# Cosine and sine products of one token tile, made in one interleaved run of matmuls instead of one after the other

## The reference

```python
def _rfs(xw, ab, AB, gs):
    dot_products = einsum('...d,rd->...r', xw, ab[:, None] * gs)
    correction = (0.5 * sum(xw * xw, axis=-1))[..., None] * (ab * ab)
    return 1.0 / sqrt(NUM_RFS) * AB * exp(dot_products - correction)
# layer 1
weights = _rfs(input_weights, ab, AB, proj_matrix)
feats = _rfs(x, ab, AB, proj_matrix)
x = layernorm(x + einsum('bsr,or->bso', feats, weights))
# layer 2
real = einsum('bti,io->bto', x, cos(theta + theta_noise))
imag = einsum('bti,io->bto', x, sin(phi + phi_noise))
x = layernorm(x + sqrt(real * real + imag * imag))
```

## Time and profile before

| | |
|---|---|
| median of 3 runs | 796.34 us (795.47 to 796.83) |
| span of the profiled execution, first to last instruction | 795.6 us |
| PE busy | 752.5 us (95% of the span), 3376 matmuls |
| DVE, ACT, POOL busy | 494.5, 366.4, 168.4 us |
| mean granted TensorE clock | 0.980 of full speed |

### The profile page before, as it was taken

One profiled execution on the slowest core, in us unless ns is written; L12 is line 12 of the kernel. 1 busy time (PEld: TensorE's weight loads), 2 busy tenths in 40 slices (PEclk: granted clock), 3 DMA queues, 4 the chain that ended last, 5 costly groups with the idle time before them and its releaser, 6 DMA issues.

```text
span 795.6 us, 10365 instructions
## 1 busy us (share of the span) xinstructions
PE 752.5 (95%) x3376; PEld 616.7 (78%) x3376; DVE 494.5 (62%) x874; ACT 366.4 (46%) x649; POOL 168.4 (21%) x300
## 2 busy tenths in 40 slices
PE   6567898999999999999999999999999999999995
PEld 5455687888888887888888887887888888888884
DVE  4288785574657557475756747574664747576464
ACT  6353644636263553526255452626445362634322
POOL 0386230120303012120301212030211203021122
PEclk9879999999999999999999999999999999999998
DMA  8663004040230403021030403104040301301001
GB/s 278 89 242 119 1 28 146 21 143 9 70 102 26 145 26 145 13 87 71 26 145 26 145 13 118 40 27 145 26 145 13 147 12 38 134 26 40 27 28 53
DMA packets 42062, 62.33 MB, mean 78 GB/s; under 512 B 11712, under 2 KB 11712, under 8 KB 42048
## 3 DMA queue, kind: packets, MB, share of 16 engines
q1 hardware_dynamic: 42048, 62.17, 24.2%
HBM read 45.35 MB, written 16.81 MB: 78 GB/s over the span
## 4 chain that ended last, share of the span: by engine, by line
PE 64%; DMA 21%; DVE 7%; ACT 4%; issue 2%; SPq 1%; POOL 0%; DVEq 0%; POOLq 0%; ACTq 0%
PE token_ps L470 14%; PE token_ps L468 14%; PE token_ps L469 14%; DMA token_norms<-norm_col 14%; DMA norm_bc<-token_norms 6%; PE project_ps L455 5%; PE project_ps L456 4%; PE project_ps L457 4%; PE token_ps L494 3%; PE token_ps L492 3%; PE token_ps L493 3%; PE turn_ps L500 2%; DVE expo L567 1%; DMA x_tok<-in_w 1%; ACT unused L316 1%
## 5 line engine op out<-in xcount | busy, mean ns | idle before, releaser
L280 POOL TENSOR_TENSOR var_eps<-mv,eps 128x1 f32<-128x1 f32 x128 | 39.7, 310 | 577.0 <-DVE mv L650 576.8
L388 ACT ACTIVATE late<-token_ps 128x512 f32<-128x512 f32 x128 | 76.1, 596 | 133.2 <-PE token_ps L470 132.8
L492 PE MATMUL token_ps<-W_hi,F_hi 128*128 128x512 f32 x256 | 100.7, 393 | 15.8 <-DVE F_lo L562 15.8
L382 ACT ACTIVATE zT_hi<-turn_ps 128x512 fp32r<-128x512 f32 x64 | 37.3, 585 | 166.6 <-PE turn_ps L500 166.6
L455 PE MATMUL project_ps<-xT_hi,gs_hi 128*128 128x512 f32 x248 | 102.7, 414 | 5.9 <-DVE expo L567 5.4
L468 PE MATMUL token_ps<-cos_hi,zT_hi 128*128 128x512 f32 x256 | 102.3, 400 | 3.1 <-DVE cos_lo L562 3.1
L470 PE MATMUL token_ps<-cos_hi,zT_lo 128*128 128x512 f32 x256 | 100.7, 393 | 0.0
L494 PE MATMUL token_ps<-W_hi,F_lo 128*128 128x512 f32 x256 | 100.4, 392 | 0.0
L493 PE MATMUL token_ps<-W_lo,F_hi 128*128 128x512 f32 x256 | 100.4, 392 | 0.0
L469 PE MATMUL token_ps<-cos_lo,zT_hi 128*128 128x512 f32 x256 | 100.3, 392 | 0.0
L468 PE MATMUL token_ps<-sin_hi,zT_hi 128*128 128x512 f32 x256 | 99.8, 390 | 0.0
(11 more groups left out here) (88 smaller groups left out, 1273.8 us busy)
## 6 DMA issues: line engine op xcount, KB each, us to landing
xT_raw<-in_xT SPq DMA_DIRECT2D x16, 1024.0 KB, 7.8
x_tok<-in_x SPq DMA_DIRECT2D x16, 1024.0 KB, 9.6
out_tokens<-o_tile SPq DMA_DIRECT2D x64, 256.0 KB, 2.9
norm_bc<-token_norms SPq DMA_DIRECT2D x17, 256.0 KB, 5.1
trig<-in_gsT SPq DMA_DIRECT2D x4, 256.0 KB, 4.7
z<-in_wT SPq DMA_DIRECT2D x4, 256.0 KB, 4.9
x_tok<-in_w SPq DMA_DIRECT2D x1, 1024.0 KB, 7.7
trig<-in_theta_noise SPq DMA_DIRECT2D x4, 256.0 KB, 6.5
```

The source lines that it names most:

```text
L388: nc.scalar.activation((re2, im2)[part][:, j % 2, :], token_ps[(2 * j + part) % 4][:, :], ACT.Square).then_inc(square_done, 1)
L492: nc.tensor.matmul(o, F_hi[:, c, cols], W_hi[:, c, :], start=(c == 0), stop=False)
```

## The change

In the steps 1 to 14 (the loop `pe.Fori(1, NB - 1)`) the eight phase products are issued as four pairs. `phase_pair(j)` goes over the chunks c once and issues for each the cosine and sine matmuls that have the same chunk of the turned tile as the stationary operand: four with `zT_hi`, two with `zT_lo`. Two PSUM banks are open at once. The semaphore `phase_done` is still raised twice a tile, by the last two matmuls. The pair waits once for what its two banks need. Step 0 and the last step keep the order of before; no other engine's code is changed.

```diff
+                def phase_pair(j):
+                    k = 2 * j % 4
+                    re_ps, im_ps = token_ps[k][:, :], token_ps[k + 1][:, :]
+                    pe.wait_ge(zT_made, C * b + j + 1 + TURN_CREDIT)
+                    if j < 2:
+                        pe.wait_ge(y_made, C * b + 2 * j + 2)
+                    else:
+                        pe.wait_ge(square_done, 2 * C * b + SQUARE_CREDIT + 2 * j - 2)
+                    for c in range(C):
+                        s, stop = slice(c * P, (c + 1) * P), c == C - 1
+                        nc.tensor.matmul(re_ps, zT_hi[:, j, s], cos_hi[:, c, :], start=(c == 0), stop=False)
+                        nc.tensor.matmul(re_ps, zT_hi[:, j, s], cos_lo[:, c, :], start=False, stop=False)
+                        nc.tensor.matmul(im_ps, zT_hi[:, j, s], sin_hi[:, c, :], start=(c == 0), stop=False)
+                        nc.tensor.matmul(im_ps, zT_hi[:, j, s], sin_lo[:, c, :], start=False, stop=False)
+                        last_re = nc.tensor.matmul(re_ps, zT_lo[:, j, s], cos_hi[:, c, :], start=False, stop=stop)
+                        last_im = nc.tensor.matmul(im_ps, zT_lo[:, j, s], sin_hi[:, c, :], start=False, stop=stop)
+                    last_re.then_inc(phase_done, 1)
+                    last_im.then_inc(phase_done, 1)
...
-                    for j, part in PHASE_ORDER_FIRST if first else PHASE_ORDER:
-                        phase(j, part)
+                    if first:
+                        for j, part in PHASE_ORDER_FIRST:
+                            phase(j, part)
+                    else:
+                        for j in range(C):
+                            phase_pair(j)
```

## The result

The changed kernel takes 812.63 us (median of 4 runs, 812.33 to 815.48) against 795.90 us for the kernel before in the same comparison (4 runs): a ratio of 1.0226, 95% interval 1.0200 to 1.0251 (an estimate from all the runs; the two medians alone give 1.0210). It is slower, by 16.7 us. Its profiled execution took 812.33 us and has a span of 810.5 us, 14.9 us more than the 795.6 of before. A run over 1.5% slower than the fastest of its kernel is left out everywhere; there was one, of 837.41 us, in the changed kernel's repeat further down.

The account below looks back on a forecast made before the run. The norms' trip through DRAM was taken to bind each step; 13 x 1.2 = 15.6 us plus 1.1 us for the last step gave a span of 812.3, plus 0.7 a forecast of 813.0 us, range 807 to 820.

Parts of the forecast that it names:

- The bound: Once a step PE waits for DVE's exponent behind the norms' trip, about 0.45 us; anything added to the trip lengthens the step.
- the norms' trip: Token norms stored to DRAM and broadcast back for DVE's exponent before project(2): store 9.93 us, load 3.36 us.
- The matmuls at 0: On PE, the new operand order and alternating banks cost 0; matmuls stay 0.227 us apart, 96 a step.
- The signal: Tile 3's cosine is ready only one matmul before sine, making output tile 1 and the norms' store 1.23 us later.
- PE's wait: PE's stand for the exponent each step, put at about 0.45 + 1.2 = 1.65 us.
- One side remark: DVE, later by the same 1.23 us, would take that delay out of its idle 2.66 us before the exponent.
- The sum: 13 trips at 1.2 us plus 1.1 us in the last step: 16.7 us on a span of 795.6, giving 812.3.
- 13 x 1.2 = 15.6: Trips behind the paired phase parts of steps 1 to 13, each lengthened by 1.2 us: 15.6 us.
- The last step: No norms there, but DVE's statistics, z and the first turn come later: +1.1 us.
- Rival 1, the clock: PE's longer stall lowers the granted clock, 1.46 us each time: 832 us in all 13 steps; chance 0.08.
- Rival 2: The norms' trip is not the last wait or shortens by as much: 796 to 800 us; no change, chance 0.05.
- Rival 3: More PE matmuls in a row with one stationary tile run faster, 786 us at 20 ns each; chance 0.04 for faster.

Follow-up runs that it names:

- the changed kernel's repeat: The changed kernel measured once more, unchanged, on the chip of a later batch: 825.12 us, ratio 1.0237 to the kernel before.
- taking the wait away: The kernel before, products apart, with DVE making output tile 1 earlier, ahead of the residual of tile 2: 793.83 us, ratio 0.9823.
- with the pairs: The changed kernel with output tile 1 made early on DVE and ACT's root moved behind the next tile's copy and sum: 794.47 us, ratio 0.9864.
- tile 3 taken back: The changed kernel with tile 3 alone back to cosine and then sine, tiles 0 to 2 still pairs: 807.97 us, ratio 0.9999.
- the cosine ahead by three: The changed kernel with each pair's last chunk issuing three cosine, then three sine matmuls: 820.64 us, ratio 1.0153 to the kernel before.
- norms first, apart: The kernel before with the token norms' store issued ahead of output tile 1's store on SP: 824.98 us, ratio 1.0216.
- norms first, pairs: The changed kernel with the token norms' store issued ahead of output tile 1's store on SP: 841.3 us, ratio 1.0403 to the kernel before.
- one signal in tile 3: The kernel before, matmuls in old order, tile 3 alone signalling cosine and sine together with its last sine matmul: 830.31 us, ratio 1.0327.
- one signal: The kernel before, matmuls in old order, every tile of steps 1 to 14 signalling both products with its last sine matmul: 833.59 us, ratio 1.0309.

## Why the prediction was right

It named 813.0 us, and 812.63 was measured. By its steps:

- **The bound.** That the norms' trip binds in each step held in both directions: 1.23 us more of it gave about 1.1 us a step, and taking the wait away gave a step of 45.45 us where it was 45.95 (12 steps from the mix at 155.07 to that at 706.49 us).
- **The matmuls at 0.** The distance is 0.227 us in the pairs, and the step without waits takes 45.45 us with the products apart and 45.45 to 45.61 with the pairs. The rule of the Trainium skill that I weighed ("TensorE: Matmul & The Clock Gate", on one weight load for many matmuls) has nothing to work on here: the profile has as many weight loads after as before, 3376.
- **The signal.** Output tile 1 was rebuilt at 3.35 us after the mix's first matmul (250.41 - 247.06), and stands at 3.35. The store of the norms came 1.23 us later, as rebuilt. The late signal alone, in tile 3 alone, reproduces the loss; tile 3 taken back removes it. PE's wait was put at 1.65 us a step, some 22 us in all, and is 20.1 us for the weight loads, 1.55 a step. One side remark was wrong: DVE did not take its delay out of its idle time ahead of the exponent, which is 2.75 us (2.66 before), because the landing it waits for moved as far.
- **The sum.** 13 x 1.2 = 15.6 was one term; the profile gives 14.1 us of idle time. The term is 1.1 us a step, not 1.2: between store and exponent the 13 trips took 13.33 us on average instead of 13.47 (from the start of the store to the start of the exponent, each of the 13). Why they were shorter stays open. The last step was put at +1.1 and is 1.54 - 0.41 = 1.13. Together 15.2, with the 0.2 given back at the start about the 14.9 of the spans. So the forecast span of 812.3 us was 1.8 too long. The time was reached from it by adding 0.7, the distance of the earlier median from one span, while the profiled execution's own time is 1.8 above its own span (812.33 and 810.5). The two errors partly cancel, so that the forecast missed by only 0.4 us is in part luck; by the spans the change cost 14.9 us, a tenth less than the 16.7 forecast.
- **Rival 1, the clock.** It did not happen in the steps 2 to 14 on the first chip, where the wait was 1.6 us at the longest, but the mechanism is real: in the kernels whose longest matmul wait was 2.2 us or more it struck in some steps, mostly at about the price given (1.46 us). A chance of 0.08 was fair for the first chip and perhaps low for that of the repeat, where the changed kernel waits up to 2.3 us and the clock fell in one step of the 13.
- **Rival 2** had hardly any ground: the trip was last in all 13 steps, and shortened by 0.14 us, not by 1.2. **Rival 3**, a gain from the shared stationary tile: none.

## What to carry to other kernels

When two products are interleaved so that they end together, the first one's result comes late by nearly the whole of the second, even if PE's own time is unchanged; ask what was done under the second one's matmuls. An engine that is 95% busy may still be held in each round by a trip of small transfers through DRAM; it shows in the chain that ended last and in a row of waits whose count is the number of rounds. And before a DMA is moved ahead of another, look up which buffer the second one frees, and when.

## What the hardware showed that I had not expected

- A 256 KB store issued 0.86 us behind the 2 KB store of the norms on the same queue was released 11 us after its issue, where the run's median is 2.9. The 2 KB store itself takes 8.0 to 11.6 us from issue to landing in that run. In the step shown the DMA engines' work was over within 2 us of either issue; what came late is the completion. Why it does, no run here shows.
- The granted clock fell to the 1.2 GHz level in some steps and not in others of the same kernel: after matmul waits up to 2.0 us in none of 13 steps (the cosine ahead by three), with the longest wait 2.2 us in one (norms first, apart) and in five (norms first, pairs), with 2.3 us in one (the changed kernel again), with 2.5 us in three (one signal in tile 3, once after a wait of 1.90), with 2.6 us in five (one signal). The length of the wait alone does not decide it.
- The norms' trip takes 13.5 us on one chip and 14.1 us on another. A chain that binds in each step makes such a difference visible: 0.6 us a trip are some 8 us of a kernel.
